# Two orderings in a graph and expert kernel: later experts' weights behind gathered rows, and a second one-hot list ahead of a norm

## The reference, cut to what matters

```python
x = x + gat(_layernorm(x), edge_index, ...)            # graph attention, two layers
x = x + ffn(_layernorm(x)[None], ...)[0]               # 8 experts, top 2, and a spectral part
x = x + rgcn_gcn(_layernorm(x), edge_index, edge_type_34, ...)
x = x + moe(_layernorm(x)[None], ...)[0]               # 8 experts, top 2, capacity 196 rows each, and a shared one
```

```python
# third block: 34 relations, each with a 768 x 768 weight
h1 = jnp.einsum('rni,rio->no', mean, W_rel) + x @ W_root + b_rgcn
# fourth block: of each expert the best 196 rows of x
order = jnp.argsort(-score, axis=1)[:, :capacity]
dispatch = flat[order]
gate = jax.nn.silu(jnp.einsum('ech,ehi->eci', dispatch, w1))
up = jnp.einsum('ech,ehi->eci', dispatch, w3)
expert_out = jnp.einsum('eci,eih->ech', gate * up, w2)
```

## Time and profile before

| | us |
|---|---|
| median of 3 runs | 1418.84 |
| lowest and highest of them | 1416.32, 1422.12 |
| the profiled execution | 1422.75 |
| its span, first to last instruction | 1421.2 |

### The profile page before, as it was taken

The page is one execution under the profiler, slowest core; times in us unless marked ns, Lnnn a source line. Parts: engine busy times, 40 slices in busy tenths (PEclk is TensorE's granted clock), DMA queues, the critical chain, the costliest instruction groups (busy, mean ns, idle before and its releaser), DMA issues.

```text
span 1421.2 us, 22852 instructions
## 1 busy us (share of the span) xinstructions
PE 1303.6 (92%) x7540; PEld 1103.8 (78%) x7540; DVE 964.3 (68%) x2158; ACT 557.1 (39%) x652; POOL 649.2 (46%) x564
## 2 busy tenths in 40 slices
PE   7988678999999989999999999999999879988997
PEld 5765568656996779999999999999866569656665
DVE  8967899888689645565656565656158875477634
ACT  0010476232433044555555555555147761212221
POOL 7025777767677633344434443544178740011121
PEclk9999697999999899999999999999999999989998
DMA  6940000020740347878787878787579863415645
GB/s 172 91 46 6 2 2 1 2 68 1 208 107 2 91 156 253 291 251 298 253 304 258 297 255 298 263 293 246 142 248 328 271 211 89 129 41 161 169 133 167
DMA packets 116402, 234.59 MB, mean 165 GB/s; under 512 B 36930, under 2 KB 57086, under 8 KB 116300
## 3 DMA queue, kind: packets, MB, share of 16 engines
q1 hardware_dynamic: 80780, 126.83, 31.0%
q0 software_dynamic: 22352, 70.40, 17.7%
q10 hardware_dynamic: 13200, 36.46, 6.9%
HBM read 195.26 MB, written 39.70 MB: 165 GB/s over the span
## 4 chain that ended last, share of the span: by engine, by line
PE 64%; DVE 21%; issue 5%; DMA 4%; ACT 3%; POOL 1%; DVEq 0%; ACTq 0%; SPq 0%; POOLq 0%
PE PS L2725 28%; PE PS L2599 4%; PE PS L2388 4%; PE PS L2713 3%; PE PS L3010 3%; PE PS L2674 3%; PE PS L2788 3%; DVE e L1321 3%; PE PS L2900 2%; PE PS L2999 2%; PE PS L2858 2%; DVE mlo L2163 2%; DVE e L1563 2%; DVE e L1600 1%; DMA pre<-z_dram,grow 1%
## 5 line engine op out<-in xcount | busy, mean ns | idle before, releaser
L815 POOL DMA_INDIRECT xg<-xn_dram,xrow x70 | 111.7, 1596 | 270.0 <-DVEq L1530 248.2
L2725 PE MATMUL PS<-whi,xhi 128*128 128x384 f32 x840 | 220.8, 343 | 1.0 <-ACTq L1103 1.0
L2725 PE MATMUL PS<-whi,xlo 128*128 128x384 f32 x840 | 215.0, 337 | 0.0
L2725 PE MATMUL PS<-wlo,xhi 128*128 128x384 f32 x840 | 213.5, 335 | 0.0
L1321 DVE TENSOR_TENSOR wlo<-raw,whi 128x2304 fp32r<-128x2304 f32 x68 | 175.2, 2576 | 39.6 <-ACTq L1086 33.7
L1084 ACT ACTIVATE whi<-raw 128x2304 fp32r<-128x2304 f32 x68 | 145.1, 2134 | 27.3 <-DMA raw<-in_L_gnn_W_rel 11.6
L2725 PEld LDWEIGHTS PS<-wlo,xhi 128*128 128x128 f32 x840 | 152.0, 188 | 0.0
L2725 PEld LDWEIGHTS PS<-whi,xlo 128*128 128x128 f32 x840 | 151.9, 188 | 0.0
L2725 PEld LDWEIGHTS PS<-whi,xhi 128*128 128x128 f32 x840 | 148.5, 189 | 1.3 <-issue 1.3
L1321 DVE TENSOR_TENSOR xlo<-PS,xhi 128x768 fp32r<-128x768 f32 x70 | 67.0, 958 | 121.6 <-ACTq L1095 114.3
L785 POOL DMA_INDIRECT zidxb<-zrow_dram,idxb x80 | 110.9, 1386 | 25.7 <-issue 25.7
(11 more groups left out here) (463 smaller groups left out, 2652.0 us busy)
## 6 DMA issues: line engine op xcount, KB each, us to landing
raw<-in_L_gnn_W_rel SPq DMA_DIRECT2D x68, 1152.0 KB
z_dram<-xn ACTq DMA_DIRECT2D x70, 384.0 KB, 7.3
gw<-in_L_gnn_W SPq DMA_DIRECT2D x2, 2304.0 KB, 27.1
fw<-in_L_ffn_w SPq DMA_DIRECT2D x8, 576.0 KB
fw<-in_L_ffn_w ACTq DMA_DIRECT2D x1, 4608.0 KB
y_dram<-yb ACTq DMA_DIRECT2D x14, 294.0 KB
xn_dram<-xn SPq DMA_DIRECT2D x10, 384.0 KB
wroot<-in_L_ffn_w SPq DMA_DIRECT2D x5, 576.0 KB, 4.9
```

The costliest lines, as they stand in the source:

```text
L815: pool.indirect_dma_start(xg[b][j][:, :], None, xn_dram, bass.IndirectOffsetOnAxis(ap=xrow[:, b, j:j + 1], axis=0)).then_inc(x_gathered[b] ...
L2725: mm = pe.matmul(slot(q)[:, s * BANK:s * BANK + HALF], a[:, k, :], wt[:, k, s * HALF:(s + 1) * HALF], start=(k == 0 and part == 0), stop=( ...
```

## The change

Three edits. SP, before it issues `load_w13(e)` for e = 3 to 7, also waits until both gathered tiles of expert e - 2 are in. DVE makes the lists of relations 2 and 3 together ahead of the norm. In exchange `relation(0, 0)` on DVE no longer makes the list of relation 3; all later ones stay where they are.

```diff
             for e in range(RING, NE):
                 sp.wait_ge(inner_full, SH + 3 * (e - RING + 1))
+                for k in range((e - RING + 1) * RT, (e - RING + 2) * RT):
+                    sp.wait_ge(x_gathered[k % 4 // 2][k % 2], 16 * (REL // 2 + (k % 2 == 0) + k // 4 + 1))
                 load_w13(e, e % RING, ld_w13[e % RING])
                 sp.wait_ge(outer_full, SH + RT * (e - RING + 1))
                 load_w2e(e, e % RING)
...
             do(dve.memset(xn_all[96:128, :, :], 0.0))
-            in_list(2, 0)
+            for b in range(2):
+                in_list(2 + b, b)
...
-            def relation(i, b, listed, more):
+            def relation(i, b, listed, more, list_coming=True):
...
-                if listed:
+                if listed and list_coming:
                     in_list(i * 2 + b + 3, 1 - b)
...
             for b in range(2):
-                relation(0, b, True, True)
+                relation(0, b, True, True, b == 1)
```

## The result

Over 22 executions of each kernel beside each other the median went from 1422.05 to 1416.72 us; the ratio of the changed kernel to the one before is 0.9957, with a 95% interval of 0.9943 to 0.9970. That is 6.1 us (4.3 to 8.1) where 6.8 were forecast; the two medians alone differ by 5.3. A second set of 12 executions on another chip gives 0.9961 (0.9943 to 0.9979).

A forecast was written before the change was run, and what follows sets the result against it. PE was taken to bound the kernel (64% of the chain), so only shortening PE waits gains much. Terms 3.1 + 0 + 3.7 = 6.8 us off the 1418.84 median gave 1412.0 us; 8-in-10 range 1408.0 to 1416.0.

The forecast's parts named there:

- SP's waits: Experts: holding back expert 3's weights lets expert 1's gather arrive earlier; 3.0 us off PE's idle plus 0.7 for the clock.
- clock term: Experts, around PE's wait for expert 1's first tile: a shorter wait takes back 0.7 us of slow work, bounds 0 and 2.0.
- Rival C: Experts: gathers are slow by their own 98 scattered rows, so waiting gains 0.5 us; total 3.6 us, 1415.2; chance 0.10.
- rival B: Experts: the clock does not fall, both slow pieces run at full clock; total 8.5 us, 1410.3; chance 0.26.
- never stands behind all of it: Experts, DMA queues: a gather beside one big load gets about half of the engines, never waiting for the whole load.
- The trace agrees: Experts: the trace was said to support queues sharing engines, with 6.8 us from gather issue to turn against 3.9 alone.
- The list, where it is taken away: Relations 1 to 3: without relation 3's list in the way PE opens earlier, relation 2 by 3.2 us; 3.1 us taken.
- From there each relation repeats the last one, shifted, and I carry 3.1 us: Relations after 3: the gain stays to the end of the block, 3.1 us, bounds 1 and 4.5 us.
- rival A: Relations: the weight stream sets the openings up to relation 6, leaving 1 to 1.5 us; total 5 us, 1413.8; chance 0.18.
- The list, where it is put: Ahead of the norm on DVE: one more list takes 3.0 us but is hidden; cost 0, upper bound 0.5 us.
- So 0.6 us of cover is left: Norm's first tile: DVE's delayed addition ends at 490.1, before PE takes that slot at 490.71.
- Rival D: Relations lock to the weight stream, each costing 0.7 us more; 21 us over 30 relations, 1433; chance 0.04.

The follow-up runs named there:

- late_list: The whole change, but with the second list made ahead of the norm's fifth tile, not the first; ratio to the kernel before 0.9963, repeated 0.9959.

## Why the prediction was right, and where not

**SP's waits** were right in every step of the sum. The gather took 3.9 us as the row of a gather beside nothing said, 3.0 us came off the wait, no weights came late, DVE was not next, and 3.7 us were forecast and 3.7 measured, with an interval of 0.8 to 6.5. The clock term of 0.7 us was a mean over two cases that both occur: the outer product behind the wait took 2.92 us in one profile and 4.4 to 4.6 in the seven others of kernels with the waits and no added work, as long as before; there only the turn got shorter, from 1.24 us to 0.7 to 0.95. Rival C (slow by its own rows) is refuted; rival B holds in one of these eight profiles. What I wrote beside the sum was wrong: "never stands behind all of it" and "The trace agrees". In the very trace that I read, the gather's first packet starts at the load's end. The term came out right because it was read from rows of a gather with and without a load and not from that rule.

**The list, where it is taken away**, has the right mechanism and a term that is too large. The 3.2 us up to relation 2 needed a list that ended at 551.89; it ended at 551.9 in the changed kernel too, and PE waited 1.66 us for it, about as computed. But I let that wait end without a price. The step "From there each relation repeats the last one, shifted, and I carry 3.1 us" failed twice. The clock fell behind the new wait, and relation 2 took 15.8 us (granted clock 0.58 over its first 3.9 us). And the list's delay is not fixed. Behind waits of 1.17 and 1.36 us the clock stayed at 1.00 and relation 2 took 14.2 us; behind waits of 1.66 to 3.82 us it took 15.5 to 16.6. On the mean over profiles 1.7 us were left, near the 1 to 1.5 that rival A had given the block, though by another way: the list stands behind the weight, and the stream itself keeps up.

**The list, where it is put**, cost about 2 us on the mean and 3 where the spectral products ran fast, not 0 with an upper bound of 0.5. The step that failed is "So 0.6 us of cover is left". It set DVE's delay against PE's arrival at 490.71, and in that one execution the spectral products ran for 9.88 us, at a clock of 0.54; in the other profiles they took 6.3 to 9.9 us. A cover that consists of slow PE work is only there when the clock is low.

So the terms, 1.7 - 2 + 3.7, give 3.4 us by stages from profiles, and the whole times give 6.1 (4.3 to 8.1); the list edit alone gives 1.7 (-0.8 to 4.2) by time and about 0 by stages. The stages' means rest on few executions of a stretch that varies by 4 us, so this gap stays open, and so does whether the list edit as made gains anything. That the total lies within 1 us of the forecast is in part luck: the two terms of the list were forecast at 3.1 and measured near 0 by stages, and only SP's waits are shown both by time and by profile. Rival D is refuted: no relation in any profile locks to the weight stream for more than a few turns.

The base was a weak point too. The forecast time of 1412.0 is 4.7 us below the measured 1416.72, which lies outside the range of 1408.0 to 1416.0: the three executions that it started from had a median of 1418.84, the 22 beside the changed kernel 1422.05. As a difference the forecast holds. And in another sense: the unchanged stretch between the relations and the experts, from the last relation product to expert 1's gather, varies from 244 to 258 us in the fourteen profiles. No argument about 3 us can be read off the difference of two spans here.

## What to carry to other kernels

When a small gather is issued just behind a large prefetch, look at the packets of both queues: it may stand behind the whole of it. Hold back the prefetch that has time, and only that one: in the profile two waits did the work of ten, and the price was nothing since the weights were wanted 37 us later. Before a step is moved under the cover of another engine's work, ask whether that work ran at the low clock in the profile; its length at full clock is the cover that can be counted on. Where PE idles for a fraction of a microsecond between light products, look at the next heavy one in the timeline: if it takes half as long again, work that nobody reads in the gap may be worth more than moving the wait.

## What the runs showed of the hardware

A gather issued 1.3 us behind a load of 1152 KB started its first packet 4.05 and 4.14 us after its issue (two profiles), 1.67 us without the load, and took no longer from there on. With a DRAM copy ahead of the load (one profile) it started after 4.43 us and moved beside the load.

The five compares of a list took 1.07 to 1.10 us wherever POOL issued no scatter beside them, and 1.26 to 1.54 us wherever at least 0.95 us of a scatter's issue (`edge_dram`) fell into them, in the lists from 480 to 620 us of all fourteen profiles; the copy before them took up to 0.6 us in place of 0.17.

The granted clock fell behind gaps of 0.85 us between light products: in `late_list` PE idled until 1305.84 at a clock of 1.00, and the clock was at 0.50 from 1307. Whether it did differed from execution to execution, and 0.8 to 1.3 us of added matmuls in each gap went with a full clock in all three profiles.
